# An LSTM recurrence on one core: gates F and O computed with units on the partitions (O in two 64-column tiles), gates I and G with rows on the partitions

## The reference

```python
xW = jnp.einsum('ntd,dk->tnk', x, Wx) + b          # Wx (256, 1024)
c0 = jnp.zeros_like(h0)                            # h0 = cond_1024, (4, 256)
def step(carry, xw_t):
    prev_h, prev_c = carry
    a = xw_t + prev_h @ Wh                         # Wh (256, 1024)
    i = jax.nn.sigmoid(a[:, 0:Hdim])
    f = jax.nn.sigmoid(a[:, Hdim:2 * Hdim])
    o = jax.nn.sigmoid(a[:, 2 * Hdim:3 * Hdim])
    g = jnp.tanh(a[:, 3 * Hdim:4 * Hdim])
    next_c = f * prev_c + i * g
    next_h = o * jnp.tanh(next_c)
    return ((next_h, next_c), next_h)
x = x + transpose(hs)                              # all 512 hidden states
```

## Time and profile before

| what | value |
|---|---|
| runs of the kernel before | 1101.48, 1100.56, 1094.28 us; median 1100.56 |
| the profiled execution: its own time | 1090.95 us |
| its span, first to last instruction | 1089.2 us |
| TensorE matmuls / weight loads busy | 64% / 53% |
| VectorE busy | 73% |
| ScalarE busy | 51% |
| mean granted TensorE clock | 0.963 of full |

### The profile page before, as it was taken

How to read it: one execution, slowest core, us unless ns; L and a number is a source line. 1 busy time by engine, 2 the same in 40 slices (tenths; PEclk the granted TensorE clock), 3 DMA queues, 4 the chain that set the end, 5 groups by cost and what they waited for, 6 DMA issues and landing times.

```text
span 1089.2 us, 88137 instructions
## 1 busy us (share of the span) xinstructions
PE 697.3 (64%) x36864; PEld 574.9 (53%) x36864; DVE 790.8 (73%) x4897; ACT 550.4 (51%) x3586; POOL 0.7 (0%) x6
## 2 busy tenths in 40 slices
PE   4666666666666666666666666667666666766664
PEld 3555555555555555555555555555555555545554
DVE  4777777777777777777776777776777777777776
ACT  2455555555545555555554555554545555455554
POOL 0000000000000000000000000000000000000000
PEclk9999999999999999999998999998999998999999
DMA  3000000000000000000000000000000000000000
GB/s 89 5 7 5 6 6 6 6 6 5 7 5 6 7 5 5 6 6 6 6 6 6 5 6 7 5 6 6 6 6 6 6 6 6 5 6 6 6 6 7
DMA packets 32110, 8.74 MB, mean 8 GB/s; under 512 B 31584, under 2 KB 31584, under 8 KB 32096
## 3 DMA queue, kind: packets, MB, share of 16 engines
q1 hardware_dynamic: 31488, 8.41, 3.5%
q10 hardware_dynamic: 608, 0.14, 0.1%
HBM read 6.43 MB, written 2.10 MB: 8 GB/s over the span
## 4 chain that ended last, share of the span: by engine, by line
DVE 51%; PE 24%; ACT 14%; issue 8%; SPq 1%; DVEq 1%; DMA 0%
DVE turned_bank L296 39%; PE gates L364 24%; DVE h_pad L314 8%; ACT tanh_o L212 8%; ACT turned_bank L215 7%; DVE scan_both L301 3%; DVE cell L307 1%; DVEq L330 1%; SPq L139 1%; DVE h_rows L270 0%; DMA wh_raw<-in_L_cond_Wh_dram 0%; SPq L143 0%; DVEq L269 0%; DVE wh L225 0%; DVE wh L222 0%
## 5 line engine op out<-in xcount | busy, mean ns | idle before, releaser
L364 PE MATMUL gates<-wh,h_pad 128*32 128x64 f32 x32768 | 591.2, 227 | 374.8 <-DVE h_pad L314 373.3
L364 PEld LDWEIGHTS gates<-wh,h_pad 128*32 128x32 f32 x32768 | 506.5, 114 | 488.3 <-DVE h_pad L314 486.4
L296 DVE STREAM_TRANSPOSE turned_bank<-gates 128x64 f32<-128x64 f32 x2048 | 478.5, 262 | 182.3 <-PE gates L364 170.0
L203 ACT ACTIVATE tanh_f<-turned_bank 128x8 f32<-128x8 f32 x512 | 90.7, 177 | 438.1 <-DVE turned_bank L296 427.6
L210 ACT ACTIVATE scan_both<-turned_bank 128x8 f32<-128x8 f32 x1024 | 185.1, 181 | 59.9 <-DVE turned_bank L296 17.3
L314 DVE SCALAR_TENSOR_TENSOR h_pad<-tanh_o,turned_bank 128x4 f32<-128x4 f32 x1024 | 132.7, 158 | 74.2 <-ACT turned_bank L215 4.6
L307 DVE TENSOR_TENSOR_SCAN cell<-scan_both 128x12 f32<-128x12 f32 x1024 | 144.0, 181 | 2.1 <-issue 0.3
L215 ACT ACTIVATE turned_bank<-cell 128x4 f32<-128x4 f32 x1024 | 143.3, 172 | 2.5 <-DVE cell L307 0.3
L346 PE MATMUL x_acc<-wx,x_units 128*32 128x128 f32 x2048 | 107.5, 285 | 9.3 <-DVE x_units L249 9.3
L212 ACT ACTIVATE tanh_o<-turned_bank 128x8 f32<-128x8 f32 x512 | 90.7, 177 | 28.9 <-DVE turned_bank L296 6.7
L216 ACT ACTIVATE half_d<-cell 128x8 f32<-128x8 f32 x512 | 100.4, 196 | 0.0
(11 more groups left out here) (24 smaller groups left out, 6.7 us busy)
## 6 DMA issues: line engine op xcount, KB each, us to landing
x_next<-in_x_dram SPq DMA_DIRECT2D x256, 8.0 KB
x_here<-in_x_dram SPq DMA_DIRECT2D x256, 8.0 KB
out_dram<-y_rows SPq DMA_DIRECT2D x256, 8.0 KB
wx_raw<-in_L_cond_Wx_dram SPq DMA_DIRECT2D x8, 128.0 KB, 3.4
wh_raw<-in_L_cond_Wh_dram SPq DMA_DIRECT2D x8, 128.0 KB, 2.7
bias_raw<-in_L_cond_b_dram ACTq DMA_DIRECT2D x4, 32.0 KB, 3.1
h_rows<-in_cond_dram ACTq DMA_DIRECT2D x4, 1.0 KB
```

The source lines that it names most:

```text
L203: nc.scalar.activation(tanh_f[:], of_step(BF, t), ACT.Tanh).then_inc(tanh_f_done, 1)
L296: nc.vector.transpose(turned[k], gates[k][:, 0:W]).then_inc(gates_turned[k], 1)
L364: last = nc.tensor.matmul(gates[k][q * R:(q + 1) * R, 0:W], h_stationary(b, t), wh[:, b, q, columns_of(k)], start=False, stop=b == M - 1, ...
```

## The change

F and O are now computed with the operands exchanged: the weights (32 units for F, 64 for O) are the stationary operand and the 4 columns of h are the moving one. The result has units on the partitions at once, and ScalarE reads it from PSUM (`f_units`, `o_units`, one bank for each half) without a turn. For O the program makes a second copy of the weights, `wh_o`, in the order that two 64-column tiles need. I and G stay by rows, with one turn for each half; the turned BB now lies in SBUF. The input part of F and O needs the layout by units too, so VectorE turns 128 columns of `x_part` (`turn_x_part`, at t = 7), `make_x_part` goes to t = 6, and the product x @ Wx goes in two pieces at t = 3 and 4. The input part of O is injected within step t = 0, between F and O. `forget` and tanh F, tanh O are split by half. On TensorE BA and F 0 of input half 0 stand ahead of the wait for h half 1; everything of BB stands behind it.

```diff
                     for m in range(M):
+                        act.wait_ge(f_done[m], now)
+                        nc.scalar.activation(tanh_f[:, m, :], f_units[m][:, t * N:(t + 1) * N], ACT.Tanh).then_inc(tanh_f_done[m], 1)
                         act.wait_ge(gates_turned[AB[m]], now)
...
-                    act.wait_ge(gates_turned[BO], now)
-                    nc.scalar.activation(tanh_o[:], of_step(BO, t), ACT.Tanh)
                     for m in range(M):
+                        act.wait_ge(o_done[m], now)
+                        nc.scalar.activation(tanh_o[:, m, :], o_units[m][:, t * N:(t + 1) * N], ACT.Tanh).then_inc(o_tanh_done, 1)
...
-                turn(BF)
                 turn(BA)
+                forget(0)
                 turn(BB)
-                forget()
-                turn(BO)
                 update(0)
+                forget(1)
                 update(1)
...
+                def units(b, bank, k, m):
+                    at = k * W + m * R
+                    for q in range(Q):
+                        last = nc.tensor.matmul(bank[q * R:(q + 1) * R, t * N:(t + 1) * N], wh[:, b, q, at:at + R],
+                                                h_at(b, t - 1), start=False, stop=b == M - 1,
+                                                tile_position=(0, q * R), skip_group_check=True)
+                    return last
+
+                def o_part(b, m):
+
+                    for p in range(Q // 2):
+                        last = nc.tensor.matmul(o_units[m][p * 2 * R:(p + 1) * 2 * R, t * N:(t + 1) * N],
+                                                wh_o[:, b, m, p * 2 * R:(p + 1) * 2 * R],
+                                                h_at(b, t - 1), start=False, stop=b == M - 1,
+                                                tile_position=(0, p * 2 * R), skip_group_check=True)
+                    return last
+
                 pe.wait_ge(h_done[0], now)
-                recur(0, BF)
+                rows(0, BA)
+                units(0, f_units[0], BF, 0)
                 pe.wait_ge(h_done[1], now)
-                recur(1, BF).then_inc(gates_done[BF], 1)
-                for k in (BA, BB, BO):
-                    recur(0, k)
-                    recur(1, k).then_inc(gates_done[k], 1)
-                if t == STEPS - 1 and ahead:
-                    pe.wait_ge(x_part_made, chunk + 2)
-                    for k in BANKS:
+                rows(1, BA).then_inc(gates_done[BA], 1)
+                units(1, f_units[0], BF, 0).then_inc(f_done[0], 1)
+                rows(0, BB)
+                rows(1, BB).then_inc(gates_done[BB], 1)
+                units(0, f_units[1], BF, 1)
+                units(1, f_units[1], BF, 1).then_inc(f_done[1], 1)
+                if t == 0:
+                    for m in range(M):
+                        inject_o(m)
+                for m in range(M):
+                    o_part(0, m)
+                    o_part(1, m).then_inc(o_done[m], 1)
+                if ahead and t in X_PRODUCT_AT:
+                    x_product(X_PRODUCT_AT.index(t), chunk + 1)
+                if ahead and t == STEPS - 1:
+                    for k in ROWS:
                         pe.wait_ge(gates_turned[k], now)
-                        inject(k)
-                if ahead and 0 <= t - FIRST_PIECE_AT < len(PIECES):
-                    x_product(*PIECES[t - FIRST_PIECE_AT], chunk + 1)
+                    for m in range(M):
+                        pe.wait_ge(tanh_f_done[m], now)
+                    pe.wait_ge(x_part_turned, chunk + 2)
+                    inject_early()
```

More of the change, by code:

```diff
@@ L26, in lstm_residual_kernel @@
     W = M * R
-    BF, BA, BB, BO = range(4)
-    BANKS = (BF, BA, BB, BO)
-    GC = len(BANKS) * W
+    BA, BB, BF, BO = range(4)
+    ROWS = (BA, BB)
+    GC = 4 * W
     AB = (BA, BB)
@@ L34, in lstm_residual_kernel @@
     WIN = R + N
-    PIECES = [(b, slice(c * GC // 2, (c + 1) * GC // 2)) for b in range(M) for c in range(2)]
-    FIRST_PIECE_AT = 3
+    X_PRODUCT_AT = (3, 4)
+    X_PART_AT = STEPS - 2
+    UNIT_COLUMNS = slice(GC - 4 * R, GC)
     ctx = ExitStack()
@@ L290, in step @@
                     nc.vector.transpose(x_units[:], x_next[:]).then_inc(x_turned, 1)
-                if ahead and t == STEPS - 1:
+                if ahead and t == X_PART_AT:
                     make_x_part(chunk + 1)
+                if ahead and t == X_PART_AT + 1:
+                    turn_x_part(chunk + 1)
                 def turn(k):
@@ L339, in _, with x_product @@
         def _(pe):
-            def x_product(b, columns, chunk):
-                opens = (b, columns) == PIECES[0]
-                if opens:
+            def x_product(b, chunk):
+                if b == 0:
                     pe.wait_ge(x_turned, chunk + 1)
                 for q in range(Q):
-                    last = nc.tensor.matmul(x_acc[q * R:(q + 1) * R, columns], x_units[:, b * R:(b + 1) * R],
-                                            wx[:, b, q, columns], start=opens, stop=b == M - 1,
+                    last = nc.tensor.matmul(x_acc[q * R:(q + 1) * R, 0:GC], x_units[:, b * R:(b + 1) * R],
+                                            wx[:, b, q, :], start=b == 0, stop=b == M - 1,
                                             tile_position=(0, q * R), skip_group_check=True)
-                if (b, columns) == PIECES[-1]:
+                if b == M - 1:
                     last.then_inc(x_acc_done, 1)
@@ L359, in step, with inject_early, rows @@
+            def inject_early():
+                for k in ROWS:
+                    inject(k)
+                for m in range(M):
+                    inject_units(f_units[m], BF, m)
             def step(chunk, t, ahead):
                 now = chunk * STEPS + (t + 1)
-                def recur(b, k):
+                def rows(b, k, columns=slice(0, W)):
                     for q in range(Q):
-                        last = nc.tensor.matmul(gates[k][q * R:(q + 1) * R, 0:W], h_stationary(b, t),
-                                                wh[:, b, q, columns_of(k)], start=False, stop=b == M - 1,
+                        last = nc.tensor.matmul(gates[k][q * R:(q + 1) * R, columns], h_stationary(b, t),
+                                                wh[:, b, q, k * W + columns.start:k * W + columns.stop],
+                                                start=False, stop=b == M - 1,
@@ L384, in _ @@
             pe.wait_ge(wx_made, M)
-            for piece in PIECES:
-                x_product(*piece, 0)
+            for b in range(M):
+                x_product(b, 0)
             pe.wait_ge(ident_made, 1)
             pe.wait_ge(zeroed, 2)
-            pe.wait_ge(x_part_made, 1)
-            for k in BANKS:
-                inject(k)
-            pe.wait_ge(wh_made, M)
+            pe.wait_ge(x_part_turned, 1)
+            inject_early()
+            pe.wait_ge(wh_made, 2 * M)
             with pe.Fori(0, CHUNKS - 1) as k:
```

60 lines of the change are left out of this document (45 added, 15 removed).

## The result

The changed kernel takes 1504.34 us (median of 4 runs, 1504.33 to 1504.50) against 1097.42 for the kernel before in the same comparison: ratio 1.373, 95% interval 1.363 to 1.383. It is 37% slower. The profiled execution took 1504.34 us too, with a span of 1502.4 us.

A forecast was written before the change was run, and what follows sets the result against it. Bound by VectorE's turns with the queue behind them and TensorE's 1.10 us burst. 1090.95 - 72 (turns) + 7 (O's injection) - 11 (clock) = 1015, plus 9.6 to the median: 1024 us; range 985 to 1290.

The forecast's parts named there:

- The clock: TensorE: loading or time with work in the array lifts the clock, half-speed steps vanish; half of 22 us taken as won.
- the sum: Chain of a step from the release by h half 1 to the next: 1.88 us at full speed, 2.02 before.
- Rival 2: TensorE stays at half clock for most steps, 2.65 us each; 1290 us given, 1389 if all steps; chance 0.27.
- hidden, with nothing to spare: x product on TensorE, 0.44 us, starts behind O near 1.2 and ends by 1.65, when h half 0 arrives.
- The full-speed step: Turn of BB, tanh IG 1 and four more tanh on ScalarE to h half 1: 1.88 us in place of 2.02.
- 72 us in all: Gain over the run from taking away the turns of BF and BO on VectorE: 0.14 us a step.
- Units of cost: TensorE at full speed: a pass (four records on four column tiles) takes 0.056 us for rows, 0.028 F, 0.056 O.
- Rival 1: Changing from 32- to 64-column tiles between F and O stops the array; step 1.97 to 2.03 us, about 1087; chance 0.20.
- The 22 us of the half-speed steps of the kernel before: About 29 steps of the kernel before ran at half clock and cost 0.77 us more each: 22 us.

The follow-up runs named there:

- e1: Changed kernel plus three unread 512-column matmuls before the first step and 256 unread moving columns in each step without input product: 1110.25 us.
- e11: e1 with each step's extra columns replaced by two matmuls of 128 stationary and 4 moving columns: 1766.16 us.
- e2: e1 with the extra matmuls before the first step but none in the steps: 1505.82 us.
- e12: e1 with 192 in place of 256 extra columns in a step: 1103.97 us.
- e10: Kernel before with only O by units in two 64-column tiles, F by rows, plus 128 extra columns in steps without input product: 1107.03 us.
- e8: Kernel before plus 64 extra columns at t = 0, 1 and 2, one turned bank moved to SBUF: 1074.21 us, ratio 0.981.
- e13: e12 with BB and F 1 of input half 0 ahead of the wait for h half 1: 1100.70 us.
- e14: e13 with F 1 ahead of BB on TensorE, both tanh F first on ScalarE, forget 1 before scan 0 on VectorE: 1111.93 us.
- e7: e1 with 256 extra columns in the steps but without the extra matmuls before the first step: 1112.30 us.
- e5: e1 with 128 in place of 256 extra columns in a step: 1113.01 us (11 runs, 1096.18 to 1158.68).
- e4: Changed kernel with O in four 32-column tiles like F: 1409.03 us (4 runs, 1360.86 to 1436.68).

## Why the prediction was wrong

- **The clock: this step failed.** I wrote that I "hold the first for likelier", that loading or time with work in the array counts and the half-speed steps vanish, and took 11 us as won. The changed kernel ran at half speed from end to end, with steps of 2.66 us for the 1.88 of the sum. e1 and e11 are the pair that settles it: the same TensorE time, given as moving columns, lifts the clock to 0.99, and given as loads leaves it at 0.51. The Trainium skill (TensorE: Matmul & The Clock Gate, "What's actually happening") says that activity releases the throttle; the runs show which activity of this kernel did. The prediction had seen that the trace before could not decide, and that streamed columns per us fall by 40%; it gave the right case 0.27 and should have given it more, since this kernel already lost its clock in plain steps.
- **Rival 2 was the right mechanism.** Its half-speed step was 2.65 us, measured 2.66, and its account (O decides, tanh O 1 waits for TensorE) is the loop that the starts in the timeline show: tanh O 1 comes 2.14 behind the release by h half 1, for 2.13 in the sum. It had two errors. It took as its time 1290, with the clock lifted by the input product in two steps of eight; all steps stayed at half, for which its sum said 1389. And 115 us were missing there: what is hidden at full speed is not at half. The product was called "hidden, with nothing to spare": at half speed it delays two steps a chunk by 0.54, and the injections cost 0.81, 1.9 us a chunk, 121 us in all. The first error alone, with the sum's own 1389, put the time out of the range of 985 to 1290.
- **The full-speed step was mis-sized too**: 1.88 forecast, 2.03 measured (e2, e12), 2.02 before. So "72 us in all" is nothing; e10 and e12 are not faster than before, and slower than e8. By the pieces of the sum: turn of BB at 0.77 for 0.71, because tanh F 0 starts at 0.48 where the sum had F 0 at 0.42 (its own units give 2 x 0.056 + 2 x 0.028 + 0.28 = 0.45); turn and hand-over 0.27 for 0.30; tanh IG 1 to tanh cell 1 0.53 for 0.46, since the scan and not ScalarE's list decides and the scan starts 0.1 after tanh IG; tanh cell, h and hand-over 0.46 for 0.41, with tanh into SBUF 0.21 long for 0.17.
- **Units of cost.** A pass of F takes 0.028 to 0.03 at full speed as taken, and O's 0.058 for 0.056. But a gate by units has twice the passes: F 8 x 0.03 against 4 x 0.056, O 8 x 0.058, twice its cost by rows. Two turns were saved on VectorE, at the price of 0.25 us more on TensorE.
- **Rival 1** exists, at about a quarter of its price: in e2's step the last pass of F starts at about 24.29 (24.20 + 0.28, less one record of 0.17 and the 0.02 within a pass) and O at 24.41, 0.12 later where its load alone needs 0.058. So the change of shape costs about 0.06 by this estimate and is hidden at full speed: tanh O does not wait. The Trainium skill (TensorEngine Tiling (Array Packing), "Key Properties") says that such a change drains the engine; the trace agrees that there is a gap, but O starts at 24.41 while the last matmul of F is shown to end at 24.48 (a modelled end), so no full drain can be read from it.
- **The 22 us of the half-speed steps of the kernel before** hold as the net gain of e8; the steps themselves had cost rather more.
- What stays open: what would bring the changed kernel's full-speed step below 2.03. e13 took TensorE's work on BB off the list of suspects and e14 forget 1, and neither gained. The path over tanh F 0 and forget 0 to the turn of BB, and the late start of the scan, were not tried.

## What to carry to other kernels

Exchanging the operands so that few columns move makes a matmul short by the profile and can cost TensorE its clock. Count moving columns per microsecond before and after, and if the trace before already has stretches at half speed, price the case that the whole kernel falls there. In these runs the loss was not undone by more loads, only by moving columns, and a few of them in idle time can pay for themselves, as in e8. Price every step at half clock too, with all that is called hidden at full clock. And before a wait is cleared as a suspect, look in the trace whether the experiment moved the instruction behind it.

## What the runs showed of the hardware

- A run that stays at half clock from its first to its last matmul has no clock record, and the profile then names 1.000. The durations tell: 310 to 315 ns is the mean of a 64-column record in runs at half speed, 219 to 226 in runs almost wholly at full. The same holds ahead of the first record of a run: e7's view shows 1.00 from the start, while 16 records of rows take 0.64 us as late as 42.86 and 0.41 from 45.18 on.
- Half speed can last: e2 fell to it after three fast steps and stayed for the rest of the run (its mean clock is 0.509), and one run of e5 stood at or near it from about 30 to 200 us with the same steps that then ran at full speed. e7, with 256 columns more in a step, got out of it without help.
- A loop whose TensorE code is a fifth longer (53248 against 44544 matmul records over the run, e4) had its instruction queue move 193 packets, with waits named "issue" of up to 5.0 us; e1, with 47656, had 12 packets, and the changed kernel 11.
